# Early-fusion block on one core: image head, batch 0, expert weights and closing loads laid out anew

## The reference, cut to what matters

```python
h = tok(x)                      # 32 images 3x96x96 -> 36 patches of 16x16, five shifted copies: 3840 features
                                # layernorm over 3840 (gamma, beta), then @ W.T (192 x 3840) + b
h = concat([h, txt], axis=1)    # 36 + 128 = 164 tokens of 192, batch 32
h = h + attn(layernorm(h))      # attn(x) = x + retrieved @ w_out.T; 8 heads, dk = dv = 64
#   keys, values and gate of batch 0 alone; fw = 0.95 fw + 0.1 g0_t k0_t (x) v0_t; retrieved_t = q_t . fw
h = h + ffn(layernorm(h))       # rms norm, softmax router over 8 experts, top 2,
#   y = sum over picked experts of comb_w * (silu(x gate_w.T) * (x up_w.T)) @ down_w.T, plus the residual
```

## Time and profile before

| what | us |
|---|---|
| three runs | 672.93, 672.92, 671.53; median 672.92 |
| the profiled execution | 671.68 |
| its span (first to last instruction) | 669.9 |
| head, 0 to 81.3 | 81.3 |
| nine patches, 81.3 to 164.1 | 82.8 |
| batch 0, 164.1 to 202.6 | 38.5 |
| attention loop, 202.6 to 313.4 | 110.8 |
| tables and rest of the units, 313.4 to 338.0 | 24.6 |
| experts, 338.0 to 625.8 | 287.8 |
| closing, 625.8 to 669.9 | 44.1 |

### The profile page before, as it was taken

The page is one execution under the profiler, slowest core; times in us unless marked ns, Lnnn a source line. Parts: engine busy times, 40 slices in busy tenths (PEclk is TensorE's granted clock), DMA queues, the critical chain, the costliest instruction groups (busy, mean ns, idle before and its releaser), DMA issues.

```text
span 669.9 us, 13234 instructions
## 1 busy us (share of the span) xinstructions
PE 541.2 (81%) x3330; PEld 500.7 (75%) x3331; DVE 402.7 (60%) x1310; ACT 305.2 (46%) x718; POOL 198.5 (30%) x293
## 2 busy tenths in 40 slices
PE   0079998997589999984679999999999999999000
PEld 0067688997487877873379999999999999999000
DVE  4590617666414777788956566566566566565197
ACT  0035992222623667767644444444444444444100
POOL 0001510000000577777403333333333333333100
PEclk9999998999599999998789999999999999999655
DMA  9999700000861122222312222222222222221695
GB/s 201 236 170 187 139 0 1 7 1 0 204 187 42 54 81 78 79 79 85 106 38 78 69 73 79 69 74 78 69 77 74 69 79 72 69 80 48 214 371 155
DMA packets 85236, 64.87 MB, mean 97 GB/s; under 512 B 42501, under 2 KB 81897, under 8 KB 84825
## 3 DMA queue, kind: packets, MB, share of 16 engines
q1 hardware_dynamic: 67160, 39.93, 26.8%
q0 software_dynamic: 8208, 16.95, 7.2%
q10 hardware_dynamic: 9840, 7.67, 4.0%
HBM read 42.61 MB, written 21.86 MB: 96 GB/s over the span
## 4 chain that ended last, share of the span: by engine, by line
PE 69%; DVE 14%; ACT 7%; DMA 4%; issue 3%; ACTq 2%; POOL 0%; POOLq 0%; SPq 0%; DVEq 0%
PE pair L750 9%; PE bank L946 5%; PE bank L942 5%; PE bank L944 5%; PE bank L945 5%; PE bank L943 5%; PE bank L953 4%; PE pair L820 4%; DVE hres L1343 4%; ACT sqjunk L471 4%; PE bank L962 4%; PE pair L962 4%; DMA bet<-in_L_tok_ln_beta 3%; PE pair L931 3%; PE bank L701 3%
## 5 line engine op out<-in xcount | busy, mean ns | idle before, releaser
L662 POOL DMA_INDIRECT disp<-xf,posu x82 | 79.8, 973 | 154.3 <-ACT xf L559 130.2
L674 POOL DMA_INDIRECT ydram<-ysb,dnow x89 | 87.3, 981 | 69.4 <-POOL dnow L671 67.1
L1308 DVE TENSOR_TENSOR hh<-sg,bank 128x384 f32<-128x384 f32 x89 | 49.3, 554 | 93.4 <-ACT sg L613 93.4
L613 ACT ACTIVATE sg<-bank 128x384 f32<-128x384 f32 x89 | 43.7, 491 | 111.5 <-PE bank L946 111.5
L750 PE MATMUL pair<-wcT,imgT 128*128 128x193 f32 x432 | 73.4, 331 | 3.8 <-DVE tmp L1063 3.8
L750 PEld LDWEIGHTS pair<-wcT,imgT 128*128 128x128 f32 x432 | 72.4, 193 | 4.1 <-issue 4.1
L942 PE MATMUL bank<-wa,xh 128*128 x178 | 67.7, 380 | 0.0
L946 PE MATMUL bank<-wa,xl 128*128 x178 | 60.3, 339 | 0.0
L944 PE MATMUL bank<-wa,xl 128*128 x178 | 60.2, 338 | 0.0
L945 PE MATMUL bank<-wa,xh 128*128 x178 | 60.0, 337 | 0.0
L943 PE MATMUL bank<-wa,xh 128*128 x178 | 60.0, 337 | 0.0
(11 more groups left out here) (228 smaller groups left out, 1253.2 us busy)
## 6 DMA issues: line engine op xcount, KB each, us to landing
xs<-disp SPq DMA_DIRECT2D x89, 96.0 KB, 1.9
img<-in_x SPq DMA_DIRECT2D x12, 392.0 KB, 8.4
yall<-ydram SPq DMA_DIRECT2D x5, 768.0 KB, 13.5
yall<-ydram ACTq DMA_DIRECT2D x5, 768.0 KB, 14.6
hres<-in_txt SPq DMA_DIRECT2D x4, 768.0 KB, 13.4
xs<-disp SPq DMA_DIRECT2D x89, 33.5 KB, 2.0
wraw<-in_L_tok_W SPq DMA_DIRECT2D x1, 2880.0 KB, 16.7
raw_gu<-in_L_ffn_gate_w SPq DMA_DIRECT2D x7, 288.0 KB, 10.7
```

The lines of the kernel that those rows point to most:

```text
L662: pool.indirect_dma_start(disp, bass.IndirectOffsetOnAxis(ap=posu[c % XBUF][:, 2 * j + k:2 * j + k + 1], axis=0), xfd[c % XBUF][:, j, :], None
L674: pool.indirect_dma_start(ydram, bass.IndirectOffsetOnAxis(ap=dnow[b][:], axis=0), ysb[b][:], None).then_inc(s_ys[b], 16)
```

## The change

It rebuilds stages 1 to 3, 5 and 6's closing, and leaves the attention and expert computations as they are. The host hands every input over in another layout (`lay_out`: copies and transposes, no arithmetic): pixels already transposed for the patch matmuls, image bands for the squares, patch weights as 30 blocks of 128 x 192, attention weights in one block, expert weights transposed.

- Head: no weight or image transposes, no borders, no strips, no products `gT`, `hT`. DVE scales 24 weight blocks by gamma and folds; PE adds up the rows of sums with 31 matmuls whose stationary operand has two columns. ACT's queue carries the parameters and constants.
- Patches: four banks for two; `patch_out(p)` waits for the squares of patches 0 to p; its second half is `patch_norm`.
- Batch 0: its text part is normalized, transposed and projected between patches 6 and 8; keys and values take two matmul steps; its 36 patch tokens are picked from `hres3` by small matmuls; no DMA is left in the stage.
- Expert weights arrive transposed. **The down weights are loaded behind the last patch** (with the main part of gate and up), straight to their place, and split in 4 units of 1152 columns in the first turns; 24 units follow, and all 28 end with the loop (`turn_units`). The rest of gate and up comes through three ring buffers of 384 columns. PE has no `expert` any more.
- `norm2(0)` moves to the end of turn 0; the table of ACT's functions is loaded ahead; the router's exponential and weights move ahead of the experts.
- Closing: `ydram` holds a partition's 41 tiles side by side; 13 loads, the first of 1, 1 and 2 tiles.

```diff
+UNITS = DOWN_UNITS + 3 * NE          # 4 + 24
+PATCH_BANK = (0, 1, 5, 6)
+LOADS = (0, 1, 2, 4, 8, 12, 16, 20, 24, 28, 32, 36, 40, 41)
 # SyncE
+            for i in range(2):
+                sp.dma_start(wraw[:, 15 * i:15 * i + 15, :], W[:, 15 * i:15 * i + 15, :]).then_inc(s_wraw[i], 16)
+            for i in range(2):
+                sp.dma_start(imgT[:, 2 * i:2 * i + 2], pixels[:, 2 * i:2 * i + 2]).then_inc(s_img[i], 16)
+            for i in range(2):
+                sp.dma_start(band[i][:], bands[:, i]).then_inc(s_band[i], 16)
...
+            sp.wait_ge(s_sq, 30)
             sp.wait_ge(s_pat, PTILES)
+            sp.dma_start(wd4[:, :, 1, :].bitcast(F32), down_w).then_inc(s_rawd, 16)
+            for e in range(NE):
+                sp.dma_start(wa5[:, e, 1].bitcast(F32), gu_w[0:P, e]).then_inc(s_rawm[e], 16)
+            sp.wait_ge(s_kv, 4 * NH)
+            for r in range(2 * NE):
+                if r >= RING:
+                    sp.wait_ge(s_lo, DOWN_UNITS + 3 * ((r - RING) // 2) + (r - RING) % 2 + 2)
+                for half in range(2):
+                    sp.dma_start(ring[r % RING][64 * half:64 * half + 64, :], gu_w[P:D, r // 2, r % 2]).then_inc(s_rawr[r % RING], 16)
 # ScalarE
+            act.dma_start(qpar[:], par).then_inc(s_par, 16)
             act.dma_start(cst[:], consts).then_inc(s_cst, 16)
...
+                    g = slice(6 * n, 6 * n + 6)
+                    ins = nc.scalar.copy(wd4[:, g, 0, :], wd4[:, g, 1, :].bitcast(F32))
...
-                if c + 1 < CHUNKS:
-                    high(2 * c)
+                for n in turn_units(2 * c):
+                    high(n)
...
+                if c == 0:
+                    norm2(0)
 # TensorE
+            pe.wait_ge(s_par, 16)
+            for k in range(WCOLS):
+                pe.matmul(bank[4][0:2, 0:D], gb[:, k, :], wraw[:, k, :], start=(k == 0), stop=False)
...
+            for p in range(1, 7):
+                patch(p)
+            pe.wait_ge(s_x0n, 1)
...
+            patch(7)
+            pe.wait_ge(s_attw, 16)
+            pe.wait_ge(s_x0T, 1)
+            for n in range(4):
+                for k in range(2):
+                    ins = project(bank[PROJ_BANK[n]][:, w * k:w * k + w], (wkT, wvT)[n // 2], 2 * (n % 2) + k, HEAD_S, SPAD)
+            patch(8)
+            for hp in range(4):
+                text_kv(0, hp)
+            pe.wait_ge(s_rsel, 1)
+            pick(EARLY[0:3])
+            pick(EARLY[3:5]).then_inc(s_pick, 1)
+            pe.wait_ge(s_rsel, 2)
+            pick(LATE[0:2])
+            pick(LATE[2:4]).then_inc(s_pick, 1)
...
-                if c + 1 < CHUNKS:
-                    expert(2 * c)
...
-                    expert(2 * c + 1)
 # VectorE
+            v.wait_ge(s_cst, 16)
+                st.mark(v.tensor_tensor(wcT[:, k:k + 6, 0:D], wraw[:, w:w + 6, :],
+                                        gb[:, w:w + 6, 0].unsqueeze(2).to_broadcast([P, 6, D]), ALU.mult))
...
                 if unit(n) is None:
+                    raw = wd4[:, 6 * n:6 * n + 6, 1, :]
+                    ins = v.tensor_tensor(raw, raw.bitcast(F32), wd4[:, 6 * n:6 * n + 6, 0, :].bitcast(F32), ALU.subtract)
```

More of the change, by code:

```diff
@@ L89, in link, with build @@
         self.wait()
-def build(nc, x, txt, gamma, beta, W, bias, w_key, w_value, w_query, w_gate, w_out,
-          norm_w, router_w, gate_w, up_w, down_w, consts, out):
+def build(nc, pixels, bands, text, W, bias, attn_w, par, norm_w, router_w, gu_w, down_w, consts, out):
     with ExitStack() as ctx:
@@ L386, in _ @@
[L386 to L392, removed]
+                sp.dma_start(x0[32 * q:32 * q + 32, :], text[32 * q]).then_inc(s_x0, 16)
@@ L503, in _ @@
[L503 to L511 removed]
+                if p + 1 < 9:
+                    squares(p + 1)
@@ new lines, in _ @@
+            for h in range(NH):
+                keys(h)
+            std_text(5)
+            nc.scalar.preload_act_table_set("sigmoid_and_others")
+            act.wait_ge(s_pick, 1)
+            add_norm(4)
+            act.wait_ge(s_k0, 5)
+            nc.scalar.copy(k0T[:, :, 0:HEAD_S], head_bank[0].rearrange("p (k s) -> p k s", k=4)).then_inc(s_k0head, 1)
+            act.wait_ge(s_pick, 2)
+            add_norm(5)
+            act.wait_ge(s_gs, 1)
+            nc.scalar.activation(kgate[:], gsum[:], ACT.Sigmoid).then_inc(s_g8out, 1)
@@ L774, in _ @@
-            ins.then_inc(s_g8, 1)
+            patch(0)
+            pe.wait_ge(s_rowm, 1)
+            pe.matmul(bank[4][:, 0:2 * D], onesf[0:2, :], rowsb[:].rearrange("p k d -> p (k d)"), start=True, stop=True
+                      ).then_inc(s_spread, 1)
+            pe.wait_ge(s_cons, 1)
+            pe.wait_ge(s_router, 1)
+            for m in range(2):
+                ins = pe.transpose(bank[7][0:DH, NE * m:NE * m + NE], rw8[:, DH * m:DH * m + DH], ident[0:NE, 0:NE])
+            ins.then_inc(s_spread, 1)
@@ new lines, in _ @@
+            text_kv(1, 1)
+            for m in range(2):
+                ins = pe.matmul(bank[3][:, 0:SPAD], wgR[:, m, :], x0T[:, m, :], start=(m == 0), stop=(m == 1))
+            ins.then_inc(s_g8, 1)
+            turn(0, 0)
+            text_kv(1, 2)
+            text_kv(1, 3)
+            for which in range(2):
+                pe.wait_ge((s_k0head, s_v0head)[which], 1)
+                pe.wait_ge(s_vvout, 6 + 2 * which)
+                for hp in range(4):
+                    head_kv(which, hp)
```

870 lines of the change are left out of this document (444 added, 426 removed).

## The result

The changed kernel takes 587.4 and 587.8 us against 672.8 (four runs, 671.5 to 672.9): 0.874 of the time before, 95% interval 0.872 to 0.876. Two further executions of it, 622.0 and 1288.8 us, were slow and are left out. The forecast was 586, range 573 to 606. The profiled execution is the one of 587.4; its span is 585.7, so 1.7 us lie beside it.

What follows compares the result with a forecast made beforehand. PE was taken to bound patches, loop and experts, the other stages no single engine. From 669.9, less 54.7 (head), 3.8 (patches), 14.5 (batch 0), 5.4 (to experts) and 8.4 (closing), it reached 586 us; range 573 to 606.

Steps and rivals of the forecast that it cites:

- Head: Up to the first patch matmul: 26.6 us instead of 81.3, set by PE's 31 sums of 18.6 us.
- Rival C: Head: PE's sums at full clock take 11 us instead of 18.6, DVE and pixels set the start; 580 us, chance 0.15.
- Patches: The nine patches: 79.0 us instead of 82.8, at 8.04 each plus 1.7 for one at a fallen clock.
- Batch 0: Last patch to first `rows`: 24 us instead of 38.5, with head keys and values as 32 matmuls of 0.2 us.
- rival B: Batch 0's stage: PE runs at 1.2 GHz throughout, +10 to +15 us; 597 us, chance 0.25.
- overlap: Batch 0: 64-row matmuls at different start partitions run together; stage up to 5 us shorter, not counted in its 24.
- Down weights: Loaded behind the last patch: landed 9.8 us after patch 8, 19 us of slack, cost 0.
- First `rows` to experts: 129.9 us instead of 135.4: POOL's scatters start at 18.4, run 104.9 without pause, 5 for landings, 1.6 for last units.
- rival D: Loop: DVE becomes the bound, its added 12.5 us of work unhidden; 598 us, chance 0.15.
- Closing: 35.7 us instead of 44.1: DVE's first instruction 2.6 us behind the first load, its 29.5 us of work unchanged.
- Experts: The experts' stretch: code unchanged, so 287.8 us stays.

Runs made afterwards that it cites:

- b1: The changed kernel with `norm2(0)` moved back from the end of turn 0 to turn 1: 581.0 us, ratio 0.866.
- b0: The changed kernel run again without any edit, on a chip like that of the result: 588.4 us, ratio 0.875.
- a0: The changed kernel run again without any edit, on another chip, where the kernel before took 714.3 us: 623.1 us, ratio 0.872.
- c1: The changed kernel with `norm2(0)` back in turn 1 and five unread matmuls in the waits of batch 0's stage, on another chip: ratio 0.856.
- a2: The changed kernel with the down weights loaded in the head and split between patches, on another chip: 628.3 us.
- b2: The changed kernel with `norm2(0)` back in turn 1 and the down weights split behind the loop: 583.9 us, ratio 0.869.
- b3: The changed kernel with the router's exponential and weights back behind ACT's loads of results: 590.6 us.
- c0: The changed kernel with `ydram`'s rows in the old order and the old view for the loads, on another chip: 626.8 us.
- c2: The changed kernel with `norm2(0)` back in turn 1 and eleven unread matmuls ahead of the experts, on another chip: ratio 0.865.

## Why the forecast was right, and where its steps failed

- **Head, 21.7 for 26.6.** PE's 31 sums took 12.3 us, not 18.6: an instruction lasted 0.53 us at first and 0.33 from 12.5 us on, and 15 of them started in the 4.7 us before that and some 45 in the next 7.5. These are the durations of 1.2 and of 2.4 GHz, though the record of the granted clock reads 1.00 for the whole head. Rival C was right on this. What then set the start was DVE, as C said, but its constants were there at 11.6, not 13. By the Trainium skill ("TensorE: Matmul & The Clock Gate", Part 1) a continuously busy PE is given the full clock; in this head the trace agrees, in the old one it did not (row 42 to 45, with L701 at 550 ns), nor does it in b1 from 104 to 116 us, busy for 12.00 of 12.00 at half of it.
- **Patches, 76.0 for 79.0.** No patch ran at the lower clock (1.7 forecast; b0 and a0 had one), and a patch took 7.88 us from start to start, for which I had 8.04. Squares and banks never held PE, as forecast.
- **Batch 0, 25.0 for 24.** Two errors of opposite sign. The 32 head matmuls of 64 rows took 2.7 us (64 instructions from 118.57 to 121.25), not 6.4, and rival B came in part: 13.7 us of the stage at 1.2 GHz, against 3.4 in c1, whose stage is 1.8 us shorter. On overlap, b1's lines, text keys (128 columns) and then head keys (48 columns):
```profile
98.70 0.27 PE L750 MATMUL pair<-k0T,aw 64*96 64x128 f32 x1
98.70 0.27 PE L750 MATMUL bank<-k0T,aw 64*96 64x128 f32 x1
98.81 0.27 PE L750 MATMUL pair<-k0T,aw 64*96 64x128 f32 x1
98.81 0.27 PE L750 MATMUL bank<-k0T,aw 64*96 64x128 f32 x1
118.79 0.24 PE L758 MATMUL bank<-k0T,aw 64*96 64x48 f32 x1
118.82 0.24 PE L758 MATMUL pair<-k0T,aw 64*96 64x48 f32 x1
118.87 0.24 PE L758 MATMUL bank<-k0T,aw 64*96 64x48 f32 x1
```
  In a patch, 193 columns of all 128 rows start every 0.164 us, which is 0.109 for 128 columns and 0.041 for 48. The text's matmuls on rows 0 to 63 and 64 to 127 start at the same moment, two in 0.11 us: they run side by side. The head's start every 0.042, which is the pace of one behind another; it was not overlap that made them cheap, but a price of 0.2 us per matmul where two instructions cost 0.084. The rule that I had set aside is that of the Trainium skill (same page, Part 3); the text's matmuls agree with it. I had also misread the trace of before: where L701 changes halves, an instruction starts 0.19 us behind the last (43.36 and 43.55) and not 0.32.
- **Down weights.** Landed at 108.7 (97.8 + 10.9; forecast 9.8 behind patch 8), first used at 127.1, 18 us of slack for 19. Nobody waited. Right, and by a2 and b2 neither other place is better.
- **First `rows` to experts, 136.2 for 129.9: the step that failed.** I wrote that "with `norm2(0)` at the end of turn 0 and no wait for turn 1's work it is some 1.5 earlier", and that POOL then runs "without a pause". The first half is right in sign: 18.0 us behind the first `rows`, against 18.4 in b1 (19.85 before). The second is wrong: I priced the wait that was added for the waiting instruction's own sake and did not ask what stands behind it on ACT, the copy for which PE and thereby the whole of turn 1 wait. b1 takes the edit back and gives 130.5. The rest of that step, POOL's chain as the path to the experts, 5 us of landings behind it, and DVE's added work hidden (no rival D), is what b1 shows: 18.4 + 107.1 + 5.0. Two terms in it cancel: the chain was to take 104.9, and the scatters are longer now (busy for 82.5 us in b1 and 83.1 in the result, against 79.8 before), while the 1.6 that I added for the last units were not needed.
- **Closing, 38.0 for 35.7.** DVE's first instruction came 3.4 us behind the first load (2.6 forecast), and it waited 1.9 us more for loads. The gain was put down to the exponential; b3 shows that it is worth 1.5 us once the loads' issue is short, and c0 that the new rows shorten the issue from 11 to 3.3 us. I had no term for that.
- **Experts** 288.7 for 287.8: they start at 1.2 GHz for 6 us (before: 3.4), behind 20 us without work for PE, which before had transposed weights there. That this is what the 0.9 us come from is not shown (c2).

## What to carry to other kernels

An instruction moved ahead in an in-order queue is to be priced by what is queued behind it while it waits: here a 2.3 us wait on ACT cost 5.3 us at the end, over PE, DVE and POOL. Where one engine's fixed chain (POOL's 82 scatters of 1.27 us) leads to the next stage, ask only for two things, when it starts and whether it is ever without work; the 12 us of work that the change added to DVE beside it stayed hidden. Matmuls that nobody reads, put into TensorE's short waits, gave back 1.8 to 3.2 us in batch 0's stage; in the long idle time ahead of the experts no gain is shown.

## What was not expected of the hardware

- TensorE busy for 12.00 of 12.00 us at the lower clock (b1, 104 to 116), with 62 instructions of small shapes; five larger matmuls ahead of and among them cut the time at that clock from 17.1 to 3.4 us.
- An indirect scatter on POOL takes 0.96 us, but 1.6 where it starts beside some of DVE's copies of 728 to 1152 columns, and then ends 0.82 to 0.84 us behind the copy (b1, b2). No run tests this.
- The issue of the same bytes by a queue depends on the DRAM side's rows: 3.3 us for seven loads whose partition reads one run of rows, 11.0 where it reads runs of 1.5 KB.
- On a0's chip the loop lost 34 us (170.3 against 136.2 from first `rows` to experts), and the kernel before took 42 us more in all (714.3 against 672.4). PE, ACT and DVE stand for 3 to 7 us in a turn with no releaser that the profile can name. Of the 34 us 3.6 lie behind the last scatter, 9.6 us before the experts instead of 6.0. Here a0, where DVE and ACT go on together 1.6 us behind the end of POOL's last scatter of a turn:
```profile
211.00 0.60 PE L774 MATMUL bank<-ident,hres 128*96 128x128 f32 x4
211.73 0.96 POOL L678 DMA_INDIRECT disp<-xf,posu  x1 [0.30 <-issue]
214.28 0.22 DVE L1246 TENSOR_TENSOR ohm<-oh,pair 128x64 f32<-128x64 f32 x1 [4.83 <-remote]
214.43 0.58 ACT L538 COPY xT<-bank 96x512 f32<-96x512 f32 x1 [3.35 <-remote]
```
  The cause stays open: no run took anything away from these turns.
